# Writing out the loop over six layers in a two-level loop nest on one Trainium2 core

## What is computed

```python
# part 1: an LSTM over 1024 time steps, batch 2, width 256
def step(carry, xw_t):
    prev_h, prev_c = carry
    a = xw_t + prev_h @ Wh                      # 256 x 1024
    i, f, o = sigmoid(a[:, :H]), sigmoid(a[:, H:2*H]), sigmoid(a[:, 2*H:3*H])
    g = tanh(a[:, 3*H:])
    next_c = f * prev_c + i * g
    return (o * tanh(next_c), next_c), o * tanh(next_c)

# part 2: six transformer layers on the LSTM's output (2 x 1024 x 256)
for i in range(6):
    x = attn_layer(shift_tokens(x), Wqkv[i], q_scale[i], k_scale[i], Wo[i]) + x
    x = ffn_layer(shift_tokens(x), ln_g[i], ln_b[i], W1[i], b1[i], W2[i], b2[i]) + x
return x_input + x
```

## Time and profile before

| what | value |
| --- | --- |
| timed runs, median (lowest to highest) | 5339.57 us (5339.14 to 5344.78) of 3 |
| profiled execution, its own time | 5329.88 us |
| its span, first to last instruction | 5326.9 us |
| mean granted TensorE clock | 0.92 of full speed |
| PE busy / PEld / DVE / ACT / POOL | 90% / 70% / 66% / 49% / 36% |
| the first stage | to about 630 us |
| seven chunks with LSTM steps | 630.39 to 4857.08 us |
| the last chunk | from 4857.08 us |
| code fetched (DMA queues of kind "instruction") | 12.81 MB of 464.73 MB |

### The profile page before, as it was taken

One profiled execution on the slowest core, in us unless ns is written; L12 is line 12 of the kernel. 1 busy time (PEld: TensorE's weight loads), 2 busy tenths in 40 slices (PEclk: granted clock), 3 DMA queues, 4 the chain that ended last, 5 costly groups with the idle time before them and its releaser, 6 DMA issues.

```text
span 5326.9 us, 206473 instructions
## 1 busy us (share of the span) xinstructions
PE 4817.3 (90%) x79632; PEld 3753.0 (70%) x79632; DVE 3541.4 (66%) x14167; ACT 2630.4 (49%) x8193; POOL 1899.0 (36%) x2070
## 2 busy tenths in 40 slices
PE   4665699999999999999999999999999999999888
PEld 1445577777777777777777777777777777776666
DVE  8665566676667667676666666676666666666554
ACT  0112355555555555555555555455455555455554
POOL 3640233333333333333333333333333333334442
PEclk6555699999999999999999999999999999999999
DMA  3020122322322322323322322332332332233431
GB/s 128 2 85 0 45 82 86 107 85 89 105 82 79 119 82 78 106 82 90 107 82 78 119 82 78 104 94 81 104 90 82 106 95 79 89 105 91 120 118 53
DMA packets 311470, 464.73 MB, mean 87 GB/s; under 512 B 213264, under 2 KB 239888, under 8 KB 297616
## 3 DMA queue, kind: packets, MB, share of 16 engines
q1 hardware_dynamic: 310544, 451.92, 28.3%
HBM read 381.93 MB, written 69.93 MB: 85 GB/s over the span
## 4 chain that ended last, share of the span: by engine, by line
PE 59%; issue 12%; DVE 9%; POOL 4%; ACT 3%; ACTq 0%; POOLq 0%; DMA 0%; DVEq 0%; SPq 0%
PE mm L914 12%; PE gates L185 12%; PE st L1026 7%; PE gates L177 5%; PE dd L1026 4%; PE st L953 3%; PE pt L1053 3%; PE pt L1061 3%; PE tt L926 2%; PE pt L967 2%; POOL va L817 2%; PE dd L983 2%; DVE pr L1398 2%; PE st L995 1%; PE st L943 1%
## 5 line engine op out<-in xcount | busy, mean ns | idle before, releaser
L802 POOL TENSOR_TENSOR turned<-raw,rotl 128x256 f32<-128x256 f32 x768 | 716.4, 948 | 1810.6 <-ACT raw L1145 1523.2
L914 PE MATMUL mm<-wqkv,xa 128*128 128x512 f32 x2304 | 1196.6, 632 | 11.1 <-DMA rot<-in_rotary 8.5
L185 PE MATMUL gates<-hp,whp 128*128 128x6 bf16 x28672 | 849.9, 166 | 23.7 <-DVE hp L230 23.4
L185 PEld LDWEIGHTS gates<-hp,whp 128*128 128x128 bf16 x28672 | 784.7, 96 | 59.0 <-DVE hp L230 31.9
L1196 ACT ACTIVATE pr<-st,nb,qn 128x128 f32<-128x128 f32 x1536 | 686.8, 462 | 134.4 <-DVE nb L1386 133.6
L192 ACT ACTIVATE state<-gsum 128x16 f32<-128x16 f32 x896 | 195.1, 218 | 987.2 <-DVE gsum L200 979.1
L914 PEld LDWEIGHTS mm<-wqkv,xa 128*128 128x128 f32 x2304 | 391.3, 196 | 249.3 <-issue 227.5
L177 PEld LDWEIGHTS gates<-hp,whp 128*128 128x128 bf16 x14336 | 425.7, 96 | 149.0 <-issue 91.0
L177 PE MATMUL gates<-hp,whp 128*128 128x2 bf16 x14336 | 485.7, 163 | 27.5 <-DVE hp L215 27.3
L200 DVE TENSOR_REDUCE gsum<-gates 128x16 f32<-128x48 f32 x896 | 182.0, 203 | 489.8 <-PE gates L185 483.2
L810 POOL TENSOR_TENSOR qn<-ss,power 128x8 f32<-128x8 f32 x192 | 321.1, 1672 | 514.5 <-DVE ss L1357 505.3
(11 more groups left out here) (135 smaller groups left out, 9796.9 us busy)
## 6 DMA issues: line engine op xcount, KB each, us to landing
wqkv<-in_Wqkv SPq DMA_DIRECT2D x288, 512.0 KB, 3.9
w<-in_W SPq DMA_DIRECT2D x48, 1364.0 KB, 5.8
wo<-in_Wo SPq DMA_DIRECT2D x48, 1024.0 KB, 5.5
w<-in_W SPq DMA_DIRECT2D x48, 768.0 KB, 4.5
kT<-k_windows SPq DMA_DIRECT2D x96, 256.0 KB, 5.2
va<-v_windows SPq DMA_DIRECT2D x96, 256.0 KB, 5.1
k_windows<-kT SPq DMA_DIRECT2D x96, 256.0 KB, 4.2
v_windows<-vb SPq DMA_DIRECT2D x96, 256.0 KB, 4.5
```

Source lines behind the costliest of these rows:

```text
L185: last = nc.tensor.matmul(g[:, m * PARTS * BATCH:(m + 1) * PARTS * BATCH], self.whp[:, p, k, m * P:(m + 1) * P], self.hp[:, k, :, :].rearr ...
L802: ins = nc.gpsimd.tensor_tensor(dst[:, :, a, :], src[:, :, 1 - a, :], tab[:, :, a, :].broadcast_to([P, 8, HALF]), ALU.mult)
L914: ins = nc.tensor.matmul(mm[c % 2][:, :], shifted(xa, y.b, k), wqkv[:, c, k, :], start=(k == 1), stop=(k == 0))
```

## The change

In each of the two places where an engine's stream loops over layers 0 to 4 by `Fori`, a Python `range` takes its place, so that the five layers are laid down one behind the other as code. With the last layer behind them a chunk is twelve slots in one body. The loop over the first seven chunks stays a `Fori`; the last chunk has no loop any more. `l` is a constant in each copy. The same edit is made to `passes` (DVE, ACT, POOL, PE) and to SP's stream. No instruction that computes or moves data is added, removed or moved to another place in its engine's order.

```diff
@@ -636,12 +636,12 @@
             with eng.Fori(0, CHUNKS - 1) as c:
-                with eng.Fori(0, DEPTH - 1) as l:
-                    layer(c, l, l + c * DEPTH, True)
+                for l in range(DEPTH - 1):
+                    layer(c, l, c * DEPTH + l, True)
                 last_layer(c, c * DEPTH + (DEPTH - 1), True)
             c = CHUNKS - 1
-            with eng.Fori(0, DEPTH - 1) as l:
-                layer(c, l, l + c * DEPTH, False)
+            for l in range(DEPTH - 1):
+                layer(c, l, c * DEPTH + l, False)
             last_layer(c, c * DEPTH + (DEPTH - 1), False)
@@ -748,12 +748,12 @@
             with sp.Fori(0, CHUNKS - 1) as c:
-                with sp.Fori(0, DEPTH - 1) as l:
-                    layer(c, l, l + c * DEPTH, True)
+                for l in range(DEPTH - 1):
+                    layer(c, l, c * DEPTH + l, True)
                 last_layer(c, c * DEPTH + (DEPTH - 1), True)
             c = CHUNKS - 1
-            with sp.Fori(0, DEPTH - 1) as l:
-                layer(c, l, l + c * DEPTH, False)
+            for l in range(DEPTH - 1):
+                layer(c, l, c * DEPTH + l, False)
             last_layer(c, c * DEPTH + (DEPTH - 1), False)
```

## The result

The changed kernel takes 5211.65 us in the median (5207.38 to 5212.24, 4 runs) against 5339.35 us (4 runs) before: ratio 0.9761, 95% interval 0.9744 to 0.9778, 2.4% faster. The prediction was 5187 us with a range of 5172 to 5220. So the time is inside the range, and the gain is 127.7 us where 152.8 had been worked out: 25 us of it are missing. The profiled execution is 5207.38 us long, its span 5205.2 us.

A forecast was written before the change was run, and what follows sets the result against it. PE was taken to set the pace, waiting for code at loop jumps; 83.2 us of standing still plus 69.6 of low clock make 152.8, so 5339.6 - 152.8 = 5186.8, about 5187 us, range 5172 to 5220.

The forecast's parts named there:

- The first term: Layer loop's end: PE's wait for code ahead of L943 goes at 28 inner jumps, 2.97 us each, 83.2 us gained.
- The second term: Slots behind the layer loop's jumps: PE's low clock goes, 21 x 2.10 + 7 x 3.64 = 69.6 us gained.
- both kinds of slot come to 48.43: Layer slots k = 0 and k = 1: without the jump both take 48.43 us, 2.10 less for k = 0.
- 1.00 in between: Layer stage: the granted clock falls six times between 630 us and the stage's end, otherwise stands at 1.00.
- rival (b): Layer's end: the standing still goes but the clock still falls, set by something else; 5256 us, chance 0.04.
- The third term: Chunk loop's end: six jumps stay on all engines; POOL and SP must newly come back over six layers; costed at nothing.
- this edge's 33 us: Chunk loop's end: upper bound if POOL's and SP's cover were gone, 6 x 5.46 us; rival 5187 to 5220, chance 0.12.
- The fourth term: Layers written out: straight code fetched as it runs adds nothing; last chunk's loop within 4 x 0.1 us either way.
- (c): Layers 0 to 4: ACT's cold code stalls at block ends, 5.46 us in each of 70 slots; 5569 us, chance 0.02.
- (d): Straight layer code: PE still stalls once a layer because its fetch can't keep up; 5330 to 5340 us, chance 0.02.

The follow-up runs named there:

- the fully written-out kernel: The changed kernel with its loop over the first seven chunks written out too, on all five engines: 5176.51 us, ratio 0.9699 to the kernel before.

## Why the prediction was right, and where not

**The first term, the standing still (83.2 us): right.** The waits ahead of L943 fell by 82 us, the six chunk edges kept theirs at 5.2 us a branch.

**The second term, the clock (69.6 us): partly wrong, in its reason and in the sum.** The low stretches at the 28 jumps are gone. But 21 new ones came at straight boundaries, 50.24 - 48.42 = 1.8 us in the slot shown. The slots that the prediction put at 48.43 us (from layer 0, k = 1, to layer 4) take 35.8 us more than that in the seven chunks, 1.7 per fall. Before, they took 154.9 us more than that, 2.1 above the two terms' 152.8. Less these 2.1 and the 1.8 by which the chunks' first slots got shorter, it is the missing 32: the seven chunks gained 120.8 us. The step that failed is the sentence "both kinds of slot come to 48.43", with the "1.00 in between" of the last part. It rested on 49 straight boundaries of the kernel before without a fall. Each of those came within three slots of a jump or of the stage's start, so no row showed many straight slots in a row, and I had no rival for it; rival (b) spoke of all of the layer's ends, not of some. The row that was held against (b), the clock at 1.00 from 4670 us on, is for the most part the last chunk, which has no LSTM steps at its slots' ends.

The reason behind the term was misread too. The prediction says of the two low stretches that the engine had stood still some 3 us before each. It had not: at 1332 us PE's idle time of 2.83 us ends at 1336.66, and the clock is low from 1334.60 on, while PE has nothing to do:

```profile
1336.66 0.63 PE L943 MATMUL st<-mask_first,ident 64*64 64x512 bf16 x2 [2.83 <-issue]
...
1334.60:1336.60 2.00, 0.00 (x0) 0.00 (x0) 0.48 (x5) 1.55 (x2) 0.00 (x0) 0.50 0.84 295
```

At the 28 inner edges the clock fell within 1.4 us after the last matmul, in the first half of the stop. So a stop of 3 us was not what the fall needed, and taking it away did not keep the clock up. It made the low stretches shorter, 3.4 us in place of 6.8 and 10.2, and fewer, 21 in place of 28.

**The third term, the chunk loop's edge at nothing: right.** SyncE and GpSimd do miss there now, and it held nobody up. The rule of the Trainium skill in "Runtime: NRT & Kernel Launch", "Instruction fetch mechanics", had both miss in the prediction's reading, since a taken branch that leaves the window must wait for its code. The trace agrees with that and not with the page's window of 512 instructions for these engines: SyncE's body of 379 and VectorE's of 421 missed. That the time lies in the range is in part luck. The range reached up to 5220 for this edge's 33 us; the 25 us above the forecast came from the clock in straight code, for which no room had been left.

**The fourth term, straight code costs nothing: right.** The last chunk's layers are 77.14 and 77.15 us, now with code packets, and the fully written-out kernel is faster still. Rivals (c) and (d) are refuted by it.

**What the prediction left out.** It read PE's branch as the whole cause. VectorE stops 4.6 us at the same place, hidden beside PE's stop and the scores. That the sum did not suffer is luck as well: the change is made on all engines. A change on PE alone would have been forecast at 5187 and is 5371. The record to look at would have been each engine's next instruction behind its branch, since VectorE's own branch is 63 ns long either way.

**The offset.** The median of the timed runs after is 4 us above the profiled execution, before it was 9.7; that is the difference between 127.7 by the medians and 122.5 by the profiled ones.

## What to carry to other kernels

A jump back whose target code must be fetched again cost PE and VectorE 4 to 5 us each, on its own; where two do it side by side, removing it from one can make things worse, so look at the next instruction behind the branch on every engine. Where PE stops, look at when the clock falls, and not only at how long it stays low: a fall at the beginning of a stop can have its reason in the work ahead of the stop. When the stops go, look again for falls in the straight code; they depend on the order of work (here eight matmuls moved by one place were worth about 20 us). Writing out is cheap where PE bounds: no variant here paid anything for longer code.

## What the runs showed of the hardware

- The clock can fall to 1.2 GHz while PE is busy without a gap: in the changed kernel PE has 12.40 us busy of 12.40 ahead of the fall at 1363.60, with many small matmuls in them. Low stretches of this kind lasted 3.4 us and cost 1.6 to 1.8 us each. They began 0.3 to 1.1 us behind the start of the slot's last weight load of L1061, whatever stood behind it. Moving eight fp32 matmuls by one place, both places ahead of that point, took them from 24 to 1. The Trainium skill, "TensorE: Matmul & The Clock Gate", section "HAM oscillation — how this bites in real kernels", puts such falls down to idle gaps of PE; here the trace does not agree, since the gap at the slot's start is 0.17 us. Which of the boundaries fall, every second or third, is left open.
- One branch hint in a loop without an inner loop took PE's jump from 5.2 to 0.36 us. On the inner one of two nested loops it left 2.1 us and cost 4.0 us at the exit.
- A stop for code need not stand in the branch's record: VectorE's branch takes 63 ns, and the 4 to 5 us come behind it.
- Which jump stopped went by the length of the body, counted in records from branch to branch or, for the chunk loop of before, along its code. On VectorE, ScalarE, GpSimd and SyncE bodies of 85 to 251 instructions came back in 0.1 to 0.3 us, and those of 379 (SyncE after), 421 (VectorE), about 490 (ScalarE) and 556 (GpSimd after) in 3 to 6 us. On PE about 1280 came back in 0.2 us, and 3459 took 3.8.
